# An attention stage's slots rearranged: output steps in pairs, a fourth buffer of exponentials, another order of tiles and units

## What is computed

```python
def attention(x, W_qkv, W_out):
    qkv = jnp.einsum('bsd,ndh->bnsh', x, W_qkv)
    q, k, v = jnp.split(qkv, 3, axis=-1)
    attn = jnp.einsum('bnqh,bnkh->bnqk', q, k) * 0.25
    attn = jax.nn.softmax(attn + causal_mask, axis=-1)
    out = jnp.einsum('bnqk,bnkh->bnqh', attn, v)
    out = out.reshape(B, -1, S)
    return jnp.einsum('bds,nhd->bsd', out, W_out)
x = layernorm(x + attention(x, W_qkv, W_out))
x = layernorm(x + feed_forward(x, ...))   # 9 paths of 256-64-256, one picked per row, mixed rows
```

## Time and profile before

| what | value |
|---|---|
| median of 3 runs | 1507.09 us (1502.43 to 1507.27) |
| the profiled execution: its own time | 1502.06 us |
| its span, first to last instruction | 1500.3 us |
| mean granted TensorE clock | 0.992 |
| TensorE busy | 1423.4 us (95%) |
| VectorE busy | 1102.5 us (73%) |
| ScalarE busy | 960.6 us (64%) |
| GpSimd busy | 431.4 us (29%) |

### The profile page before, as it was taken

One profiled execution on the slowest core, in us unless ns is written; L12 is line 12 of the kernel. 1 busy time (PEld: TensorE's weight loads), 2 busy tenths in 40 slices (PEclk: granted clock), 3 DMA queues, 4 the chain that ended last, 5 costly groups with the idle time before them and its releaser, 6 DMA issues. The chain is left out here.

```text
span 1500.3 us, 25145 instructions
## 1 busy us (share of the span) xinstructions
PE 1423.4 (95%) x8234; PEld 656.3 (44%) x8282; DVE 1102.5 (73%) x2647; ACT 960.6 (64%) x2121; POOL 431.4 (29%) x561
## 2 busy tenths in 40 slices
PE   7999989999999999999999999999988999999995
PEld 4665543333333333333333333333324666566654
DVE  3225658888888888888888888888733888878775
ACT  4655447777777777777777777777775445455532
POOL 3443232122133133133133133123243262122312
PEclk9999999999999999999999999999999999999998
DMA  7899674223643843842842842842714521110001
GB/s 224 265 296 292 205 217 111 87 63 95 156 89 95 181 92 90 185 93 85 190 93 80 195 94 74 200 95 66 143 23 130 92 85 57 43 56 28 15 29 43
DMA packets 166752, 178.20 MB, mean 119 GB/s; under 512 B 26397, under 2 KB 135784, under 8 KB 166632
## 3 DMA queue, kind: packets, MB, share of 16 engines
q1 hardware_dynamic: 158184, 168.31, 44.2%
q10 hardware_dynamic: 8448, 8.39, 1.7%
HBM read 109.79 MB, written 66.06 MB: 117 GB/s over the span
## 5 line engine op out<-in xcount | busy, mean ns | idle before, releaser
L975 ACT ACTIVATE a_probs<-a_ps_s 128x512 f32<-128x512 f32 (+3 forms) x1536 | 648.0, 499 | 232.2 <-PE a_ps_s L1077 228.5
L176 DVE CUSTOM_DVE_ANT_0 h_space<-a_ps_m,a_causal 128x640 f32<-128x640 f32 (+5 forms) x624 | 530.3, 888 | 94.5 <-PE a_ps_m L150 91.1
L1077 PE MATMUL a_ps_s<-s_qs,s_ks 99*128 99x512 bf16 (+3 forms) x1536 | 405.6, 329 | 6.5 <-ACT a_probs L975 4.7
L150 PE MATMUL a_ps_m<-s_ks,s_qs 96*128 96x512 bf16 (+3 forms) x1440 | 347.1, 326 | 9.1 <-DVE a_mx L176 2.3
L925 POOL TENSOR_SCALAR_AFFINE_SELECT a_probs<-a_probs 128x512 f32<-128x512 f32 x256 | 163.0, 637 | 664.6 <-ACT a_probs L975 664.6
L1035 PE MATMUL a_ps_o<-a_probs,s_vq 128*32 128x512 f32 (+3 forms) x3072 | 327.6, 497 | 10.1 <-POOL a_probs L925 4.2
L1077 PEld LDWEIGHTS a_ps_s<-s_qs,s_ks 99*128 99x128 bf16 x1536 | 137.0, 97 | 330.7 <-ACT a_probs L975 241.6
L150 PEld LDWEIGHTS a_ps_m<-s_ks,s_qs 96*128 96x128 bf16 x1440 | 122.6, 98 | 157.8 <-issue 57.9
L1547 PE MATMUL f_ps_o<-f_w,f_hm 128*128 128x256 f32 (+1 forms) x640 | 151.5, 385 | 0.9 <-DVE f_y L1454 0.9
L1547 PEld LDWEIGHTS f_ps_o<-f_w,f_hm 128*128 128x128 f32 (+1 forms) x640 | 121.5, 192 | 27.6 <-issue 8.4
L545 PE MATMUL p_ps_qk<-p_x_t,p_wqk 128*128 128x512 f32 x256 | 120.5, 600 | 0.1
(11 more groups left out here) (137 smaller groups left out, 1310.6 us busy)
## 6 DMA issues: line engine op xcount, KB each, us to landing
qk_parts<-h_space SPq DMA_DIRECT2D x64, 384.0 KB, 4.0
s_qs<-qk_parts SPq DMA_DIRECT2D x192, 128.0 KB, 2.8
s_ks<-qk_parts SPq DMA_DIRECT2D x192, 128.0 KB, 2.8
v_rows<-h_space SPq DMA_DIRECT2D x16, 896.0 KB, 6.1
s_vq<-v_rows SPq DMA_DIRECT2D x32, 448.0 KB, 4.5
f_x_in<-in_L_attn_x_dram ACTq DMA_DIRECT2D x16, 512.0 KB, 6.7
heads_out<-a_o_sb SPq DMA_DIRECT2D x128, 64.0 KB
f_x_in<-in_L_attn_x_dram SPq DMA_DIRECT2D x8, 1024.0 KB, 8.8
```

Source lines behind the costliest of these rows:

```text
L150: last = pe.matmul(out, self.qs[0:TROWS, j, h, q], self.ks[0:TROWS, j, h, s:s + wide], start=k == 0, stop=mask is None)
L176: taken = dve.tensor_tensor_reduce(out=shown[:, i % 2, k * CHUNK:k * CHUNK + width], in0=row, in1=self.causal[:, SEQ - width:SEQ], scale=1 ...
L975: act.activation(probs[:, st % PB, h, 0:width], ps_s[:, n % BANKS, 0:width], ACT.Exp, scale=SCALE).then_inc(exps[h % 2], 1)
L1077: pe.matmul(ps_s[:, n % BANKS, 0:width], ks[0:MROWS, j, h, kt * P:(kt + 1) * P], qs[0:MROWS, j, h, q0:q0 + width], start=True, stop=True)\
```

## The change

- `STEPS`: key tiles are visited in the order 0, 3, 1, 2 in the first half of the queries and 1, 0, 5, 4, 7, 3, 6, 2 in the second. The first step of each half opens the accumulation, the last closes it.
- `GROUPS`: outputs of the first four steps are issued singly as before, those of the second half two steps together; `OUT_AT` has eight places instead of 12, and the last pair is issued at `n` = 5 of the next slot.
- `PB` = 4. The space comes from `Head`: its input `aw` now lies where `mixa` is written later; the last stage has two `f_aw` buffers of its own. In the projection stage the second half of V lies in `a_in` instead of the same space (`v_sb` is a list of two; the lines of that are left out below, as is the signature of `project_stage`).
- `UNITS` are in an order that mixes long and short ones, `UNIT_AT` has new places. The unit of tile 0 stays the third. The projection stage uses the same list for the units of the first two slots.
- `keep_o` follows exponential 6 and 29 (`KEEP_AT`) instead of steps 0 and 4 (exponentials 3 and 19).

```diff
--- before.py
+++ after.py
@@ -42,11 +42,11 @@
 PIECE = [(0, 1, 2, 3), (4, 5, 6, 7)]
 EPS = 1e-5
 
-UNITS = [((h,), qt) for qt in range(CT, TILES) for h in range(QUAD)]
-UNITS += [(tuple(range(h, h + 2)), qt) for qt in (3, 2) for h in range(0, QUAD, 2)]
-UNITS += [(tuple(range(QUAD)), 1)]
+UNITS = [((0,), 5), ((1,), 7), ((0, 1, 2, 3), 0), ((3,), 6), ((2,), 7), ((2,), 4), ((3,), 4), ((2,), 5),
+         ((0,), 7), ((2,), 6), ((1,), 5), ((3,), 5), ((0,), 4), ((0,), 6), ((0, 1, 2, 3), 1), ((2, 3), 3),
+         ((1,), 6), ((0, 1), 3), ((2, 3), 2), ((1,), 4), ((3,), 7), ((0, 1), 2)]
 TURN = 2
-UNITS.insert(TURN, (tuple(range(QUAD)), 0))
+assert UNITS[TURN][1] == 0
 NU = len(UNITS)
 RBANKS = 2
 LOADS = 16 * (2 * len(TERMS) + 1)
...
@@ -235,13 +236,12 @@
         wqk = sb("p_wqk", [P, KC, QKM, P], F32)
         x_rows = x_in[:, :, :].rearrange("p (c t) d -> p c t d", c=CHUNKS)
         x_t = sb("p_x_t", [P, CHUNKS, KC, CHUNK], F32)
-        cuts = [0]
-        for size in (CHUNKS * QKM * PARTS * CHUNK // 2, CHUNKS * QUADS * CT * QUAD * VW):
-            cuts.append(cuts[-1] + size)
-        parts, v_sb = (space[:, a:b] for a, b in zip(cuts, cuts[1:]))
-        parts = parts.bitcast(BF16).rearrange("p (c m i q) -> p c m i q", c=CHUNKS, m=QKM, i=PARTS)
+        held = CHUNKS * QKM * PARTS * CHUNK // 2
+        parts = space[:, 0:held].bitcast(BF16).rearrange("p (c m i q) -> p c m i q", c=CHUNKS, m=QKM, i=PARTS)
+        v_size = QUADS * CT * QUAD * VW
+        v_sb = [v.rearrange("p (j t v) -> p j t v", j=QUADS, t=CT)
+                for v in (space[:, held:held + v_size], a_in[:, :, :].rearrange("p t d -> p (t d)")[:, 0:v_size])]
         rest = sb("p_rest", [P, QKM, CHUNK], F32)
-        v_sb = v_sb.rearrange("p (c j t v) -> p c j t v", c=CHUNKS, j=QUADS, t=CT)
         ps_t = pb("p_ps_t", [P, CHUNK], F32)
         ps_qk = pb("p_ps_qk", [P, QKM, CHUNK], F32)
         ps_v = pb("p_ps_v", [P, 2, D], F32)
...
@@ -732,11 +732,11 @@
         def sem(name):
             return ctx.enter_context(nc.semaphore(name))
 
-        sizes = [TILES * D, TILES * D, KC * (SEQ + 2), KC * SEQ, KC * SEQ]
+        sizes = [TILES * D, KC * (SEQ + 2), KC * SEQ, KC * SEQ]
         self.space = sb("h_space", [P, sum(sizes)])
         ends = [sum(sizes[:i + 1]) for i in range(len(sizes))]
-        aw, x1, x1_t, xm, mixa = (self.space[:, b - a:b] for a, b in zip(sizes, ends))
-        self.aw = aw.rearrange("p (t d) -> p t d", t=TILES)
+        x1, x1_t, xm, mixa = (self.space[:, b - a:b] for a, b in zip(sizes, ends))
+        self.aw = mixa.rearrange("p (t d) -> p t d", t=TILES)
         self.x1 = x1.rearrange("p (t d) -> p t d", t=TILES)
         self.x1_t = x1_t.rearrange("p (k s) -> p k s", k=KC)
         self.xm = xm.rearrange("p (k s) -> p k s", k=KC)
...
@@ -843,16 +843,20 @@
         ident, ident16, mask16 = consts
         qs, ks, vq, loaded = quads
         o_sb, o_kept, out_sent = residual.o_sb, residual.o_kept, residual.out_sent
-        STEPS = [(c, kt) for c in range(CHUNKS) for kt in range(CT * (c + 1))]
+        STEPS = [(0, 0), (0, 3), (0, 1), (0, 2), (1, 1), (1, 0), (1, 5), (1, 4), (1, 7), (1, 3), (1, 6), (1, 2)]
         NST = len(STEPS)
 
 
 
-        UNIT_AT = [0, 2.5, 4, 6, 7, 11.5, 13.5, 16, 19, 20.5, 22, 23.5, 25, 27, 29.5, 32, 33, 35, 36.5, 39.5, 43, 44.5]
-        OUT_AT = [4, 8, 12, 15, 19, 23, 29, 32, 35, 40, 44, 47]
-        PB = 3
+
+        GROUPS = [(0,), (1,), (2,), (3,), (4, 5), (6, 7), (8, 9), (10, 11)]
+        UNIT_AT = [0, 2.5, 4, 7.5, 8, 11.5, 13, 16, 18.5, 20, 22.5, 24.5, 26.5, 28, 30.5, 33, 35.5, 38.5, 40, 42.5, 44, 47]
+        OUT_AT = [5, 10, 14, 21, 25, 33, 41, 47]
+        KEEP_AT = (29, 6)
+        PB = 4
         BANKS = 3
-        assert NU % 2 == 0 and QUAD * NST % BANKS == 0
+        assert NU % 2 == 0 and QUAD * NST % BANKS == 0 and NST % PB == 0
+        assert all(STEPS[st][0] == st // CT or st >= CT for st in range(NST)) and STEPS[CT][1] <= CT
 
         probs = sb("a_probs", [P, PB, QUAD, CHUNK], F32)
         ps_s = pb("a_ps_s", [P, BANKS, CHUNK], F32)
...
@@ -974,10 +978,11 @@
                                 act.wait_ge(scores, QUAD * NST * t + n + 1)
                                 act.activation(probs[:, st % PB, h, 0:width], ps_s[:, n % BANKS, 0:width],
                                                ACT.Exp, scale=SCALE).then_inc(exps[h % 2], 1)
-                            if st == 0 and not (isinstance(t, int) and t == 0):
-                                keep_o(t - 1, (j - 1) % 2, 1, sent_before(*((b, j - 1) if j else (b - 1, QUADS - 1))))
-                            if st == CT:
-                                keep_o(t, j % 2, 0, sent_before(b, j))
+                                if n == KEEP_AT[1] and t:
+                                    keep_o(t - 1, (j - 1) % 2, 1,
+                                           sent_before(*((b, j - 1) if j else (b - 1, QUADS - 1))))
+                                if n == KEEP_AT[0]:
+                                    keep_o(t, j % 2, 0, sent_before(b, j))
 
                 turn(0)
                 for b in range(1, BATCH):
...
@@ -1029,12 +1034,13 @@
                     if kt >= c * CT:
                         own = sum(k >= cc * CT for cc, k in STEPS[:st + 1])
                         pe.wait_ge(masked, TILES * t + own)
-                    if kt == 0:
+                    first, last_one = (st in (0, CT)), (st in (CT - 1, NST - 1))
+                    if first:
                         pe.wait_ge(o_kept, CHUNKS * t + c)
                     for h in range(QUAD):
                         last = pe.matmul(ps_o[h * OW:(h + 1) * OW, off:CHUNK], vblocks(vq)[:, j, kt, VBLOCK[h] * HD:(VBLOCK[h] + 2) * HD],
                                          probs[:, st % PB, h, 0:width],
-                                         start=(kt == 0), stop=(kt == CT * (c + 1) - 1))
+                                         start=first, stop=last_one)
                     last.then_inc(pv_done, 1)
 
                 def turn(b, last):
...
@@ -1055,14 +1061,15 @@
                             if n == 2 * QUAD and after and not more:
                                 pe.wait_ge(maxima.rows_max, NU * SLOTS)
                                 maxima.turn(pe, ps_x, (t + 1) % 2)
-                            for st in range(NST):
-                                if OUT_AT[st] == n and st:
-                                    products(t, j, st - 1)
-                                    if not after and st <= CHUNKS * KC:
-                                        head.transposes(pe, ps_m[:, (st - 1) // RBANKS, (st - 1) % RBANKS, :],
-                                                        (st - 1) // KC, (st - 1) % KC, ident)
-                                elif OUT_AT[st] == n and before:
-                                    products(t - 1, (j - 1) % QUADS, NST - 1)
+                            for g in range(len(GROUPS)):
+                                for st in GROUPS[g - 1]:
+                                    if OUT_AT[g] == n and g:
+                                        products(t, j, st)
+                                    elif OUT_AT[g] == n and before:
+                                        products(t - 1, (j - 1) % QUADS, st)
+                                if OUT_AT[g] == n and 0 < g <= CHUNKS * KC and not after:
+                                    head.transposes(pe, ps_m[:, (g - 1) // RBANKS, (g - 1) % RBANKS, :],
+                                                    (g - 1) // KC, (g - 1) % KC, ident)
                             for i in range(NU):
                                 if more and UNIT_AT[i] == n + 0.5:
                                     rows(t + 2, jm, i)
...
@@ -1082,7 +1089,8 @@
                 for b in range(1, BATCH - 1):
                     turn(b, False)
                 turn(BATCH - 1, True)
-                products(SLOTS - 1, QUADS - 1, NST - 1)
+                for st in GROUPS[-1]:
+                    products(SLOTS - 1, QUADS - 1, st)
 
 
 def feed_stage(nc, residual, head, weights, w_loaded, out):
...
@@ -1113,7 +1121,7 @@
         ident16 = sb("f_ident16", [P, P], BF16)
         widen = sb("f_widen", [P, PATHS + 1, DM], BF16)
 
-        aw = [head.aw, sb("f_aw", [P, TILES, D], F32)[:, :, :]]
+        aw = [sb(f"f_aw{e}", [P, TILES, D], F32)[:, :, :] for e in range(2)]
         x1 = [head.x1, sb("f_x1", [P, TILES, D], F32)[:, :, :]]
         xm = [head.xm, sb("f_xm", [P, KC, SEQ], F32)[:, :, :]]
         x1_t, mixa, half = head.x1_t, head.mixa, head.half
```

More of the change, by code:

```diff
@@ L206, in send, with project_stage @@
                          self.mrow[:, i, :]).then_inc(self.max_sent, 16)
-def project_stage(nc, x, w_qkv, qk_parts, v_rows, residual, maxima, weights, stored, head, x_in,
+def project_stage(nc, x, w_qkv, qk_parts, v_rows, residual, maxima, weights, stored, head, inputs,
                   consts, quads):
@@ L224, in project_stage @@
         ident, ident16, mask16 = consts
+        x_in, a_in = inputs
```

(8 more changed lines are left out.)

## The result

| | before | changed |
|---|---|---|
| median of 4 runs | 1507.13 us (1502.43 to 1507.27) | 1441.95 us (1439.80 to 1445.97) |
| profiled execution, own time | 1502.06 us | 1445.97 us |
| its span | 1500.3 us | 1444.3 us |

The ratio is 0.9579, with a 95% interval of 0.9557 to 0.9601: 4.2% or 63 us faster (the two medians lie 65 us apart). The forecast was 1468, the range 1448 to 1492.

The account below looks back on a forecast made before the run. TensorE was taken to bound the attention stage: slots go from 28.28 to 27.14 us (joins 0.73, waits 0.41), thirty save 34.2 and the last two 4, so 1502.06 becomes 1464, plus 4 for the median: 1468 us, range 1448 to 1492.

Parts of the forecast that it names:

- The join, 0.18 us of at most 0.24: Second-half output steps: each of four pairs saves 0.18 us by following as a pass does, 0.73 us a slot.
- Rival (1): Output pairs: the join saves nothing, only waits move; 1486 us, as a median 1490; chance 0.13.
- Waits fall by 0.4 us a slot: TensorE's waits in an attention slot: 0.31 + 0.5 - 0.4 us less, from 1.3 to 0.9.
- the split's 0.31: Fifth unit, behind VectorE's split: its wait of 0.31 us goes, since the last output group now lies between.
- the narrow tiles' 1.0 us: Small waits at narrow key tiles: with each beside a wide one, half of 1.0 us goes, 0.5.
- 0.4 us of new wait at n = 25 to 33: New tight place ahead of the first pair: ScalarE needs 4.2 us against TensorE's 3.8; 0.4 us charged.
- Pairs do not starve the others: ScalarE and VectorE during a pair of 2.0 us: slack and work behind each pair cover it; costed at nothing.
- rival (3): Behind each pair: starved ScalarE leaves TensorE 0.5 us of wait; slower, 1540 us, as a median 1544; chance 0.08.
- The fourth buffer adds and saves nothing by itself: Fourth buffer of exponentials: it adds no work, and ScalarE's wait ends halfway in a pair.
- The last two slots gain 4 us: Last two slots, without units: outputs no longer wait for masks; net -2 us each, bounds 0 and -4.
- GpSimd, SyncE, projection, tail: nothing: Work outside the slots' main terms: masks, loads and tail cost nothing; projection within +-2 us.
- Rival (5): Attention slots: waits almost gone, 1.0 us less a slot, last two 4 each; 1442 us, median 1446; chance 0.07.

Follow-up runs that it names:

- experiment 1: The changed kernel with one score between the two steps of each pair; 1467.81 us, ratio 0.9772 to the kernel before.
- Experiment 5: The kernel before with four buffers of exponentials and second-half outputs in pairs, old places and orders; 1532.18 us, ratio 1.0178.
- 9: The changed kernel with both key tiles and units in the order of before; 1499.36 us, ratio 0.9962 to the kernel before.
- experiment 4: The kernel before with the changed memory layout and four buffers of exponentials, single outputs, old places and orders; 1504.81 us, ratio 1.0008.
- experiment 3: The changed kernel with the units of maxima in the order of before at the new places; 1464.30 us, ratio 0.9749.
- Experiment 7: The changed kernel with single outputs in the last two slots only; 1439.84 us, ratio 0.9567 to the kernel before.
- experiment 10: The changed kernel with single outputs in the last two slots and VectorE's reciprocal behind unit 18; 1435.03 us, ratio 0.9534.

## Why the prediction was right and wrong

*TensorE is the bound, and work taken off it shortens the slot.* Right: experiment 1 gives the 0.93 us back in full in an undisturbed slot.

*The join, 0.18 us of at most 0.24.* The mechanism was right, the term too small: 0.24 by the pair's own rows, 0.23 by experiment 1. Four a slot over 30 slots are 29 us where the sum had 22. I had taken off the upper bound what a change of pass cost within a step (0.45 where 0.43 is the bare work); between joined passes it is 0.437 on average. Rival (1), that nothing is saved, falls, and with it the rule on weight loads by which it was built: in "TensorE: Matmul & The Clock Gate", Part 3, "What overlaps and what doesn't", the Trainium skill lets a weight load overlap only other row groups; here column tiles over the same rows are loaded at 688.47 and 688.90 while passes run, and the passes follow each other at 0.437 us for 512 columns. Its drain at a change of tiling mode ("TensorEngine Tiling (Array Packing)", Key Properties) is in line with the 0.24 us, and the estimate of two drains of 128 cycles, 14 us in all, was half of what was saved. The change of mode is here always a change from bf16 to fp32 as well, and no run tells which of the two costs the time.

*Waits fall by 0.4 us a slot.* This is the step that failed: they fell by 1.05, from 1.31 to 0.26. The 0.65 us more than forecast is 19 us over 30 slots, most of the 25 us by which the term of the thirty slots was too small (34 forecast, 59 measured). Its first part, the split's 0.31, was right. Its second, that half of the narrow tiles' 1.0 us would stay, and its third, 0.4 us of new wait at n = 25 to 33, were both wrong. I charged the third because ScalarE's sum over that stretch (4.2 us) was above TensorE's (3.8), as if each stretch began with both engines level. ScalarE enters it ahead, and unit 15 covers the copy in full: the trace has 0.09 us there.

*Pairs do not starve the others.* Right for the changed kernel, but only with its order. I had costed it at nothing by slack over a whole slot and by the scores and units behind each pair, as if any order had them, and gave rival (3) 0.08. Experiment 5 shows rival (3) in the flesh with the same slack, and 9 shows half of it still there. Not the slack but the order was the cover. That I listed the orders as a separate item with a gain of their own was the real fault: of the waits that the orders and places removed (from 3.2 to 0.2), 1.9 were made by the pairs.

*The fourth buffer adds and saves nothing by itself.* Right, by experiment 4; whether pairs need it was not tested.

*The last two slots gain 4 us.* Wrong: 1.2 at full clock, by experiments 3 and 4, and in the profiled executions +0.3, because of the half clock. Experiment 7 gains another 2.3 by undoing the pairs there.

*Each fourth slot.* Missed: before, it was 0.3 us longer than the others, now 0.76. VectorE's 1.2 us of extra work stood ahead of units of 640 columns and now stands ahead of one of 896 and one of 1024; with the old order of units, in experiment 3, it costs nothing. In the changed kernel it is 6 x 0.45 = 2.7 us more than before, and experiment 10 gets that and a little more back (3.7 us).

*GpSimd, SyncE, projection, tail: nothing.* Right: the transpose of the projection stage stands at 174.15 us (174.02 before) and the first of the slots at 224.54 (224.46).

In all: thirty slots -59 instead of -34, last two +0.3 instead of -4 (1.6 of that the clock), the rest +2.4, where the granted clock was lower: -56 between the two profiled executions, -65 between the medians, since the one profiled before lay 5 us under its median and the changed one 4 us above its own. Rival (5) came near by luck in part: its waits (1.0 us a slot less) were right, its join was too small and its 8 us for the last two slots too large.

## What to carry to other kernels

An engine that is full and serves two others in turns can be given longer blocks only if what stands around each block is refitted: the same pairs cost 27 us in the old order, and with the new one the kernel gained 63. Slack over a whole period says nothing about it; count what the others hold in their buffers when a block starts, and what they find when it ends. Measure waits as distances between starts minus known work, since the idle rows of weight loads did not move when the waits fell by four fifths. And where the mix of work changes, as in the last two slots here, the schedule needs another variant.

## What the runs showed of the hardware

- Going from bf16 matmuls over the full array to fp32 ones in 32-column tiles and back costs 0.23 to 0.24 us. It is the same in pairs with a narrow step: 512 with 128 columns take 1.22 us from first matmul to the next instruction where two single steps take 1.00 + 0.36, and 512 with 512 take 1.85 where two take 2.00, 0.14 to 0.15 less in both, plus the 0.095 ahead of the second. Between two steps in the tiled form it costs nothing that can be seen, though every pass has its own weights.
- Waits of the two orders added up almost exactly (0.94 and 0.92 us for the units, 1.07 and 1.05 for the tiles), which I had not expected of engines that wait for one another.
- The granted clock was 0.50 in a few short stretches of each trace. One of them, on a pair of output steps, made the pair last 3.57 us instead of 1.92 and the last two slots 1.6 us longer (52.27 against 50.63 us; with single outputs 49.93 against 48.35). Before two traces are compared by a few microseconds, such stretches have to be looked for in both.
